# Scores in bursts of three, later gates and alternating banks in a fused attention and feed-forward layer

## The reference, cut to what matters

```
xn = layernorm(x)                                  # 1024 tokens x 256
s  = attention(xn) @ Wproj.T + bproj               # softmax(q k^T / 4) v per head
h  = gelu(xn @ proj1.T + b1)                       # 1024 x 1024
y  = h @ proj2.T + b2                              # 1024 x 256
out = x + s * silu(y)
```

## Time and profile before

| | |
|---|---|
| Median of 3 runs | 136.43 us (135.93 to 136.46) |
| The profiled execution | 136.42 us, of which span of the core 134.5 us |
| TensorE busy | 123.0 us (91%) |
| VectorE busy | 89.3 us (66%) |
| ScalarE busy | 75.7 us (56%) |
| GpSimd busy | 50.8 us (38%) |
| Start of the first score unit S0 | 43.94 us |
| Start of the first transposed unit ST0 | 84.63 us |
| First exponential | 85.17 us |

### The profile page before, as it was taken

How to read it: one execution, slowest core, us unless ns; L and a number is a source line. 1 busy time by engine, 2 the same in 40 slices (tenths; PEclk the granted TensorE clock), 3 DMA queues, 4 the chain that set the end, 5 groups by cost and what they waited for, 6 DMA issues and landing times.

```text
span 134.5 us, 2614 instructions
## 1 busy us (share of the span) xinstructions
PE 123.0 (91%) x980; PEld 93.4 (69%) x980; DVE 89.3 (66%) x178; ACT 75.7 (56%) x115; POOL 50.8 (38%) x53
## 2 busy tenths in 40 slices
PE   6769979999997999999999999698999999999970
PEld 5449868988897889887677787465665566666450
DVE  0558974610000799999996999667668756858983
ACT  3044457879992011109467605649869787987710
POOL 3259203999995000002755660069604000004400
PEclk9999999999999999999999999999999999999998
DMA  4699879999999999200000000800000110110103
GB/s 123 201 407 425 224 163 150 153 158 152 172 181 184 163 170 174 51 0 2 5 0 0 0 15 10 301 11 7 17 0 0 44 39 0 44 41 2 44 2 117
DMA packets 7553, 13.29 MB, mean 99 GB/s; under 512 B 1012, under 2 KB 2676, under 8 KB 7284
## 3 DMA queue, kind: packets, MB, share of 16 engines
q1 hardware_dynamic: 7108, 12.85, 43.0%
q10 hardware_dynamic: 432, 0.27, 0.7%
HBM read 5.51 MB, written 1.05 MB: 49 GB/s over the span
## 4 chain that ended last, share of the span: by engine, by line
PE 70%; DVE 10%; ACT 8%; DMA 5%; issue 5%; SPq 1%; ACTq 0%; DVEq 0%
PE bank L590 48%; PE bank L706 10%; PE bank L658 6%; PE bank L678 6%; DMA wqkv_raw<-wqkv 5%; DVE negm L506 4%; ACT PT L431 4%; DVE cd L523 1%; DVE yh L548 1%; ACT cTh L443 1%; ACT xTh L375 1%; DVE rc L526 1%; DVE fin L565 1%; SPq L259 1%; ACT wqh L365 0%
## 5 line engine op out<-in xcount | busy, mean ns | idle before, releaser
L506 DVE TENSOR_REDUCE negm<-bank 128x4 f32<-128x1024 f32 x32 | 37.0, 1216 | 18.7 <-PE bank L658 18.6
L431 ACT ACTIVATE PT<-bank 128x1024 f32<-128x1024 f32 x32 | 30.7, 1019 | 6.6 <-PE bank L678 6.6
L340 POOL TENSOR_TENSOR hTl<-hG,hTh 128x512 fp32r<-128x512 f32 x16 | 20.3, 1289 | 26.1 <-ACT hTh L417 26.0
L350 POOL TENSOR_TENSOR bg<-gate,bps 128x256 f32<-128x256 f32 x8 | 5.9, 741 | 34.7 <-DVE gate L471 25.8
L706 PE MATMUL bank<-PT,VA 128*17 128x256 f32 x256 | 16.9, 382 | 0.0
L437 ACT ACTIVATE th<-yh 128x256 f32<-128x256 f32 x8 | 3.3, 418 | 23.0 <-DVE yh L548 23.0
L590 PE MATMUL bank<-w2h,hTh 128*128 128x256 f32 x64 | 14.8, 313 | 1.2 <-ACT VA L398 0.8
L678 PE MATMUL bank<-qs,ks 50*128 50x256 f32 x128 | 13.1, 312 | 1.7 <-ACT PT L431 1.7
L590 PEld LDWEIGHTS bank<-w2h,hTh 128*128 128x128 f32 x64 | 9.7, 190 | 6.5 <-issue 4.6
L413 ACT ACTIVATE hG<-bank,b1s 128x512 f32<-128x512 f32 x16 | 11.0, 689 | 5.5 <-PE bank L590 5.5
L523 DVE STREAM_TRANSPOSE cd<-bank 128x256 f32<-128x256 f32 x16 | 7.2, 447 | 10.5 <-PE bank L706 10.5
(11 more groups left out here) (72 smaller groups left out, 205.5 us busy)
## 6 DMA issues: line engine op xcount, KB each, us to landing
qs<-stage SPq DMA_DIRECT2D x12, 256.0 KB, 11.8
ks<-stage SPq DMA_DIRECT2D x12, 256.0 KB, 17.9
w_raw<-w SPq DMA_DIRECT2D x2, 1024.0 KB, 9.5
xs<-x SPq DMA_DIRECT2D x4, 256.0 KB, 5.9
xb<-x SPq DMA_DIRECT2D x1, 1024.0 KB, 5.3
out<-fin SPq DMA_DIRECT2D x8, 128.0 KB, 1.7
wqkv_raw<-wqkv SPq DMA_DIRECT2D x3, 256.0 KB, 6.9
wps<-wp SPq DMA_DIRECT2D x8, 32.0 KB, 8.2
```

The source lines that it names most:

```text
L340: nc.gpsimd.tensor_tensor(hTl[:, n % FC, :], hG[:, n % FC, :], hTh[:, n % FC, :].bitcast(f32), ALU.subtract).then_inc(h_lo, 1)
L350: nc.gpsimd.tensor_tensor(bg[:, u % 2, :], gate[:, u, :], bps[:], ALU.mult).then_inc(bg_done, 1)
L431: nc.scalar.activation(PT[:, w % 4], scores_of(*s), ACT.Exp).then_inc(exp_done, 1)
L506: nc.vector.tensor_reduce(negm[:, j, :, :, s[1] % 2, b].rearrange("p q a -> p a q"), scores_of(*s), axis=AX.X, op=ALU.max, negate=True).th ...
```

## The change

Four edits, all in the order of the steps and in where results lie; the arithmetic is the same, and so is the number of instructions on every engine.

1. The units S are issued in 11 bursts (ten of three, the last of two), with the same filler spread over 11 stretches in place of 16. The list from the last step before the S stage on is, with filler first and units behind it: F2 0.0-0.2 | S0-2; F2 0.3, 1.0-1.2 | S3-5; F2 1.3, 2.0, 2.1 | S6-8; F2 2.2-3.1 | S9-11; F2 3.2, 3.3, F1 8 | S12-14; F1 9 | S15-17; F1 10, 11 | S18-20; F1 12, 13 | S21-23; F1 14, 15, MT0 | S24-26; F2 4.0-4.2, MT1 | S27-29; F2 4.3, 5.0, 5.1 | S30, 31; F2 5.2, then ST0. (F2 1.3 is part 3 of tile 1.) MT0 and MT1 now stand ahead of a burst's units.
2. `finish_gate` leaves the F2 step and has steps GATE of its own: gate 0 behind ST1 (in VectorE's queue behind the last reduction), gates 1 to 6 behind PV 1 to 6. Gate 7 stays. `yh` is written into the gate's own place, `th` gets five slots, and the waits of `yh` go.
3. In the ST stage MT2 and MT3 stand ahead of the F2 part of their group.
4. Banks: tiles 4 to 7 alternate between 7 and 6; MT0 keeps to the alternation, MT1 and MT3 take bank 6, MT2 bank 7. `ones` shares memory with `cd`.

```diff
+BURST = 3
-    share = sum(w for _, w in filler) / len(PAIRS)
-    at = 0
-    for n in range(len(PAIRS)):
+    bursts = [range(n, min(n + BURST, 2 * len(PAIRS))) for n in range(0, 2 * len(PAIRS), BURST)]
+    share = sum(w for _, w in filler) / len(bursts)
+    at, turn = 0, [[], []]
+    for n, burst in enumerate(bursts):
         while filler and at < (n + 1) * share - 0.5:
...
-        order += [("S", 2 * n), ("S", 2 * n + 1)]
-        if n >= 2 and PAIRS[n - 2][1] == B - 1 and PAIRS[n - 2][0] < 2:
-            order.append(("MT", PAIRS[n - 2][0]))
+        order += [("MT", j) for j in turn.pop(0) if j < 2] + [("S", u) for u in burst]
+        turn.append([PAIRS[u // 2][0] for u in burst if u % 2 and PAIRS[u // 2][1] == B - 1])
...
         if g >= 1:
             order.append(("PV", g - 1))
+        if g in (0, 2, 3, 4, 5, 6, 7):
+            order.append(("GATE", max(g - 1, 0)))
+        if g in (1, 2):
+            order.append(("MT", g + 1))
 
         if g >= 1 and (j == 0 or b <= 1):
             order.append(ffn.pop(0))
-        if g in (1, 2):
-            order.append(("MT", g + 1))
         if g == GROUPS - 2:
-            order.append(("GATE",))
+            order.append(("GATE", TT - 1))
...
-        yh = at("yh", [P, 2, E], f32, wq_at + 8 * KB)
-        th = at("th", [P, 2, E], f32, wq_at + 10 * KB)
+        th = at("th", [P, 4, E], f32, wq_at + 8 * KB)
...
-                elif (kind in ring and not (kind == "MT" and n > late)) or (kind == "F2" and s[1] < TT // 2):
+                elif kind == "F2" and s[1] >= TT // 2:
+                    home[s] = (7 - s[1] % 2,)
+                elif s == ("MT", 2):
+                    home[s] = (7,)
+                elif s == ("MT", 0) or (kind in ring and kind != "MT") or kind == "F2":
                     home[s] = (5 + turn % 3,) if n < first_s and kind != "F2" else (6 + turn % 2,)
                     turn += 1
-                elif kind == "F2" or s[:2] == ("PJ", TT - 1):
+                elif kind == "MT" or s[:2] == ("PJ", TT - 1):
                     home[s] = (6,)
...
                     act.wait_ge(yh_done, u + 1)
-                    if u >= 2:
-                        act.wait_ge(gate_done, u - 1)
-                    nc.scalar.activation(th[:, u % 2, :], yh[:, u % 2, :], ACT.Tanh).then_inc(th_done, 1)
+                    if u >= 5:
+                        act.wait_ge(gate_done, u - 4)
+                    nc.scalar.activation(th_of(u), gate[:, u, :], ACT.Tanh).then_inc(th_done, 1)
...
                     dve.wait_ge(f2_made, u + 1)
-                    if u >= 2:
-                        dve.wait_ge(gate_done, u - 1)
-                    nc.vector.scalar_tensor_tensor(yh[:, u % 2, :], bank_of("F2", u, 0)[:, 0:E], 0.5, b2s[:],
+
+                    nc.vector.scalar_tensor_tensor(gate[:, u, :], bank_of("F2", u, 0)[:, 0:E], 0.5, b2s[:],
                                                    ALU.mult, ALU.add).then_inc(yh_done, 1)
-                    if u >= 1:
-                        finish_gate(u - 1)
                 elif s[0] == "GATE":
-                    finish_gate(TT - 1)
+                    finish_gate(s[1])
```

More of the change, by code:

```diff
@@ L154, in layer_kernel @@
         gate = at("gate", [P, TT, E], f32, wq_at)
-        yh = at("yh", [P, 2, E], f32, wq_at + 8 * KB)
-        th = at("th", [P, 2, E], f32, wq_at + 10 * KB)
+        th = at("th", [P, 4, E], f32, wq_at + 8 * KB)
         VA = at("VA", [P, TT, NH, VW], f32)
         ident = at("ident", [P, P], f32)
-        ones = at("ones", [2, SQ], f32)
+        th_more = at("th_more", [P, E], f32)
         warm = at("warm", [P, HALF // 2], f32, stage_at)
+        cd_at = used[0]
         cd = at("cd", [P, 2, SQ], f32)
+        ones = at("ones", [2, SQ], f32, cd_at)
         b1s = at("b1s", [P, FC], f32)
@@ L202, in layer_kernel @@
         pj_made, gated, fin_done = sem("pj_made"), sem("gated"), sem("fin_done")
-        first_s, late = order.index(("S", 0)), order.index(("F2", TT // 2, 0))
+        first_s = order.index(("S", 0))
         ring = ("QK", "V", "F1", "MT")
@@ L245, in bank_of, with th_of @@
             return bank[:, home[s][0], :]
+        def th_of(u):
+            return th[:, u % 5, :] if u % 5 < 4 else th_more[:]
         def scores_of(*s):
@@ L470, in finish_gate @@
                 dve.wait_ge(th_done, u + 1)
-                nc.vector.scalar_tensor_tensor(gate[:, u, :], th[:, u % 2, :], 1.0, yh[:, u % 2, :],
+                nc.vector.scalar_tensor_tensor(gate[:, u, :], th_of(u), 1.0, gate[:, u, :],
                                                ALU.add, ALU.mult).then_inc(gate_done, 1)
```

## The result

The changed kernel took 139.18 us in the median of 4 runs (138.55 to 139.50), the kernel before 136.19 (135.93 to 136.46): ratio 1.021, 95% interval 1.017 to 1.026. The sign was forecast and, for the way to the first exponential, the mechanism; the size was not: +1.0 us was predicted, +3.0 measured, above the upper end of the range (138.5). Measured a second time the two kernels gave 1.018 (1.014 to 1.021), 139.04 against 136.53. Medians here are over all executions of a kernel, ratios over those within 1.5% of its fastest.

What follows compares the result with a forecast made beforehand. VectorE, with TensorE nearly as full, was taken to bound the S stage, TensorE the ST stage, ScalarE's table load joining them. +1.13 - 0.45 + 0.33 = +1.0 us on 136.42 gave 137.4 us, range 135.5 to 138.5.

Steps and rivals of the forecast that it cites:

- Bursts, TensorE's side: S stage: five fewer round trips of 0.39 us save TensorE 2.0 us, 1.5 of it given back in waits.
- The ledger and the wait at MT0: S stage, burst-by-burst times: VectorE idles 1.5 us for MT0's copy; table load then holds the first exponential, +1.13 us.
- Gate 4: ST stage, VectorE: gate 4 ahead of `yh` of tile 6 delays the tanh and exponentials behind it, +0.33 us.
- Group 0, -0.45: ST stage: `ctxn` of group 0 no longer runs beside GpSimd's gate work, shortening a TensorE wait, -0.45 us.
- the rivals: Whole kernel: savings arrive, 135.5 us, chance 0.18; MT0's wait harmless, 136.55, 0.22; late gates collide, 139.4, 0.08.
- That of colliding gates: ST stage: gates 1 to 6 pull GpSimd beside VectorE's normalisation; +2 us beyond the sum, 139.4 us, chance 0.08.

Runs made afterwards that it cites:

- before_look1: The kernel before the change, without edits, profiled again in one execution: 135.89 us.
- gates_only: Changed kernel with pairs, banks and MT places put back, memory layout and late gates kept: 137.03 us, ratio 1.004 to the kernel before.
- mt0_first: Changed kernel with MT0's copy ahead of F1 15's gelu and copy in ScalarE's queue alone: 136.81 us, ratio 1.002 to the kernel before.

## Why the prediction was wrong

By its steps:

- **Bursts, TensorE's side**: right. Twelve matmuls and the way out take 0.91 us (45.88 to 46.79), forecast 0.90. Five round trips of 0.39 are saved and 1.5 us of them lost in waits: S17 begins at 65.44, 1.59 behind S15 (63.85), where 0.47 would do (forecast 1.1 of wait); S8 waits another 0.35.
- **The ledger and the wait at MT0**: right, 1.50 us idle before `mm` and the first exponential behind the table load; from tile 0 to it +1.2 us (forecast +1.13), and with the two places in ScalarE's queue undone it is gone (-1.1 and -0.7).
- **Gate 4**: right in size, not in place. Gates alone take 49.1 us behind the first exponential, the kernel before 48.8 in two of three profiles: +0.3 (forecast +0.33). But the sign that the prediction gave for it, 0.5 us idle before the ST matmuls that had 0.16, did not come; they have 0.19:

```profile
104.99 0.19 PEld L599 LDWEIGHTS bank<-wph,cTl 128*128 128x128 f32 x1 [0.24 <-DVE cTl L566]
106.00 0.50 PE L687 MATMUL bank<-qs,ks 50*128 50x256 f32 x4 [0.19 <-ACT PT L443]
```

  The late tanh also holds ScalarE's copy `cTh` behind it, VectorE's `cTl` follows that, and TensorE waits for `cTl` in the projection. From one ST step to the next it is 2.87 us (102.44 to 105.31), 2.56 before (100.57 to 103.13).

- **Group 0, -0.45**: this term failed. The collision of `ctxn` with GpSimd (0.87 us in the earlier trace rows) was in that execution only, one of three. In both later profiles `ctxn` of group 0 takes 0.29 and `yh` comes 0.93 behind the transposition, not 1.52. What differs is the order of two starts: in the profile before GpSimd's `xb` began at 89.44 and `ctxn` at 89.45; in before_look1 both began at 89.58, and there it was `xb` that took longer (0.88 us for 0.73):

```profile
89.44 0.73 POOL L352 TENSOR_TENSOR xb<-xb,bg 128x256 f32<-128x256 f32 x1
```

```profile
89.58 0.29 DVE L530 TENSOR_TENSOR ctxn<-cd,rc 128x128 f32<-128x128 f32 x1
89.58 0.88 POOL L352 TENSOR_TENSOR xb<-xb,bg 128x256 f32<-128x256 f32 x1
```

  The first to the fifth exponential take 5.41 us there and 5.43 in the changed kernel, not 6.00: in these executions there was nothing to gain. With this, the part that the steps explain is +1.2 and +0.4 (49.2 against 48.8), 1.6 us.

- **The clock**: the missing step, put at nothing without a reason, and the larger one. I put the 1.13 us in as a delay that only shifts what follows. But TensorE stands still more in it, 1.15 us behind ST1 and 0.9 before S28 and S29, and in three of four profiles the clock went to half for 3.4 us, at 0.75 to 1.3 us each time. By these profiles that is about 0.8 us in the mean (1.2, 0.75 and 1.3 over four), and 1.6 + 0.8 = 2.4 us; the two measurements gave 3.0 and 2.5, so that 0.1 to 0.6 us stay open. The run with useless matmuls, 1.0 us faster, is the direct evidence. The mean granted clock of the executions behind the ratios points the same way, though it holds the early stretch too: 0.966 for the changed kernel run again and 0.976 for the kernel before beside it, 0.978 with the useless matmuls and 0.981 for the kernel before beside those.

The page "TensorE: Matmul & The Clock Gate" of the Trainium skill, section "HAM oscillation — how this bites in real kernels", tells of a kernel in which TensorE's wait between groups of matmuls brings back the lower clock for the group behind it. The kind of loss agrees with the profiles here. But the page's waits are for transfers and longer than the 1.15 us behind ST1, and taken by its rule they would have left the clock as it was; the half clock in three of four profiles decides against that. I had used another section of that page and not weighed this one, although the change lengthens the wait behind ST1 from 0.65 to 1.15 us.

Of the rivals none came true. That of colliding gates had the nearest time (139.4) by the wrong mechanism: with the gates back the kernel isn't faster, and gates alone cost 0.3 us in the profile, 0.5 in the median.

What stays open: how still TensorE must be for the clock to fall. The kernel before waits 0.65 and 0.41 us at the same place and kept full clock in three profiles, gates_only 0.86 and 0.42 with full clock in its one. mt0_first waits 1.15 and 0.41 us there, as long as the changed kernel: its first exponential comes only 0.1 us later than before, but ST0 comes 1.3 us ahead of it and not 0.5. Its one profile fell to half, yet its median is near that of the kernel before. And the first profile of the changed kernel, with the same waits as the others, kept full clock.

## What to carry to other kernels

Where every engine walks one list of steps, a step moved for one engine is moved in all their queues; ask of each queue which instruction now stands ahead of which, and reorder only the queue that suffers. A wait on the path to the end costs its length and, where TensorE stands still in it, can cost clock in the work behind it (here 0.75 to 1.3 us): price it with both. Before counting a gain from a slow row, see whether the row is slow in another execution as well.

## What was not expected of the hardware

- Seven matmuls of no use (1.1 us of TensorE) in a wait for the first exponential lowered the median from 139.0 to 138.0 us, the ratio from 1.018 to 1.009.
- The granted clock rose to full between 12.1 and 16.3 us in fourteen profiles of kernels with the same first 42 us, and tile 0 began between 41.6 and 44.4 us; a single profile can't be compared with another from time zero.
- The same elementwise instruction took 0.29 or 0.87 us, beside GpSimd's work that began within 0.01 us of it, by which of the two came first.
